# A two-layer mixture kernel: the lower layer's TensorE loop cut from four steps to two and begun two steps early

## The reference, cut to what matters

```python
def reference(x, ctx_1024, ...):                 # x: 32 x 64 x 512, ctx: 32 x 1601 x 512, all float32
    x = x + cross_attention(layernorm(x), ctx_1024)
    x = x + self_attention(layernorm(x))         # 16 heads, causal
    return x + ffn(layernorm(x))

def kmoe(x_flat, W_router, A, B, scale, bias, d_in1, d_in2, d_out1, d_out2, top_k):
    logits = x_flat @ W_router.T                 # 64 experts
    vals, idx = jax.lax.top_k(logits, top_k)     # top_k = 2
    probs = jax.nn.softmax(vals, axis=-1)
    xs = x_flat.reshape(-1, d_in1, d_in2)
    Y = jnp.einsum('nkoi,nij,nkpj->nkop', A[idx], xs, B[idx])
    out = jnp.einsum('nkop,nk->nop', Y, probs).reshape(-1, d_out1 * d_out2)
    return out * scale + bias

def ffn(x):                                      # x.reshape(-1, 1024): 1024 tokens of 32 x 32
    h = kmoe(x, W_up, ..., 32, 32, 64, 64, 2)    # the upper layer: 32 x 32 -> 64 x 64
    h = jax.nn.gelu(h, approximate=False)
    return kmoe(h, W_down, ..., 64, 64, 32, 32, 2)   # the lower layer: 64 x 64 -> 32 x 32
```

## Time and profile before

| | us |
|---|---|
| median of 3 runs (lowest, highest) | 1310.11 (1308.2, 1310.57) |
| the profiled execution | 1309.42 |
| its span in the profile | 1307.6 |
| PE busy in the span | 1223.3 (94%) |
| DVE busy | 802.9 (61%) |
| ACT busy | 440.8 (34%) |
| POOL busy | 277.3 (21%) |

### The profile page before, as it was taken

One profiled execution on the slowest core, in us unless ns is written; L12 is line 12 of the kernel. 1 busy time (PEld: TensorE's weight loads), 2 busy tenths in 40 slices (PEclk: granted clock), 3 DMA queues, 4 the chain that ended last, 5 costly groups with the idle time before them and its releaser, 6 DMA issues.

```text
span 1307.6 us, 63760 instructions
## 1 busy us (share of the span) xinstructions
PE 1223.3 (94%) x28879; PEld 803.6 (61%) x28879; DVE 802.9 (61%) x1603; ACT 440.8 (34%) x894; POOL 277.3 (21%) x470
## 2 busy tenths in 40 slices
PE   9999999999999999999999999786898989789995
PEld 6864333333333333776667766566787878689995
DVE  5566677777777672465555656364756657357774
ACT  2323211321122112221222212225555537257772
POOL 1100000000000001121222212014352515236663
PEclk9999999999999999999999999899999999989996
DMA  8887999899989992411011110400412203644333
GB/s 296 283 258 231 306 298 307 276 314 299 313 268 319 300 305 65 109 65 64 1 65 64 64 48 0 130 34 34 161 65 96 90 39 154 230 166 113 113 65 65
DMA packets 66133, 211.56 MB, mean 162 GB/s; under 512 B 12240, under 2 KB 28624, under 8 KB 51568
## 3 DMA queue, kind: packets, MB, share of 16 engines
q1 hardware_dynamic: 66032, 210.16, 48.6%
HBM read 172.37 MB, written 37.75 MB: 161 GB/s over the span
## 4 chain that ended last, share of the span: by engine, by line
PE 81%; DVE 9%; issue 4%; POOL 2%; ACT 1%; DMA 1%; SPq 1%; POOLq 0%; DVEq 0%; ACTq 0%
PE ps L714 14%; PE ps L563 10%; PE ps L1087 8%; PE ps L2244 5%; DVE arena L575 5%; PE ps L2276 5%; PE ps L2195 5%; PE ps L235 4%; PE ps L1201 4%; PE ps L1108 4%; PE ps L478 3%; PE ps L2173 2%; PE ps L704 2%; PE ps L2289 2%; PE ps L2230 2%
## 5 line engine op out<-in xcount | busy, mean ns | idle before, releaser
L575 DVE STREAM_TRANSPOSE arena<-arena 128x448 f32<-128x448 f32 (+1 forms) x512 | 263.4, 578 | 98.5 <-PE ps L563 79.5
L563 PE MATMUL ps<-arena 32*64 32x400 f32 (+1 forms) x4096 | 202.8, 506 | 2.6 <-DVE arena L575 1.8
L714 PE MATMUL ps<-arena 128*64 128x512 f32 x832 | 189.2, 598 | 0.0
L563 PEld LDWEIGHTS ps<-arena 32*64 32x64 f32 x4096 | 74.9, 130 | 99.5 <-issue 50.7
L714 PEld LDWEIGHTS ps<-arena 128*64 128x64 f32 x832 | 55.5, 136 | 121.3 <-issue 112.0
L598 ACT ACTIVATE arena<-ps,arena 128x384 f32<-128x384 f32 x64 | 36.3, 582 | 276.4 <-DVE arena L589 276.4
L1087 PE MATMUL ps<-arena 128*128 128x256 f32 x512 | 115.3, 383 | 0.8 <-ACT arena L1022 0.8
L1087 PEld LDWEIGHTS ps<-arena 128*128 128x128 f32 x512 | 97.3, 192 | 17.5 <-issue 3.3
L887 POOL TENSOR_TENSOR arena<-arena 128x1024 f32<-128x1024 f32 x8 | 19.0, 2370 | 405.7 <-PE ps L714 405.7
L2091 ACT COPY arena<-ps 128x512 f32<-128x512 f32 x128 | 75.1, 587 | 75.5 <-PE ps L2244 49.1
L1922 DVE SCALAR_TENSOR_TENSOR arena<-ps,arena 128x512 f32<-128x512 f32 x64 | 69.9, 1117 | 38.3 <-PE ps L2230 37.9
(11 more groups left out here) (161 smaller groups left out, 1895.0 us busy)
## 6 DMA issues: line engine op xcount, KB each, us to landing
arena<-ctx SPq DMA_DIRECT2D x64, 1024.0 KB
arena<-ctx SPq DMA_DIRECT2D x32, 768.0 KB
arena<-q_n SPq DMA_DIRECT2D x64, 256.0 KB, 11.2
h_n<-arena SPq DMA_DIRECT2D x16, 1024.0 KB, 4.4
arena<-h_n SPq DMA_DIRECT2D x16, 1024.0 KB, 7.8
arena<-x SPq DMA_DIRECT2D x16, 512.0 KB, 4.3
arena<-ctx SPq DMA_DIRECT2D x32, 256.0 KB
x_n<-arena SPq DMA_DIRECT2D x16, 512.0 KB, 3.5
```

The lines of the kernel that those rows point to most:

```text
L563: last = pe.matmul(ps[b * SEQ:(b + 1) * SEQ, tb, 0:WIDTH[tb]], qs[p % 2][r, db, b * SEQ:(b + 1) * SEQ], z[r, at % RING, b, 0:WIDTH[tb]], s ...
L575: vec.transpose(z[:, at % RING, :, g * 224:g * 224 + nt * 32].rearrange("p b (j t) -> p b j t", t=32), slots[slot_of(k)][:, :, 0:nt, db * ...
L714: last = pe.matmul(ps[b * SEQ:(b + 1) * SEQ, OB, :], probt[:, j, b * SEQ:(b + 1) * SEQ], slot[:, b, jj, :], start=j == 0, stop=j == TILES - 1)
```

## The change

- **Main loop of the lower layer.** The four-step body becomes a two-step body, run 7 and then 21 times, over steps -2 to 53. `first_dn(0)` and `first_dn(1)` are no longer written out ahead; the loop begins two steps earlier, and its first two `second_dn` work on nothing. 56 of the 64 units lie in the loop; it is left when the last is gathered. Then come four laps of two steps without units (three before).
- **Early units.** `EARLY` is 8; they run as a loop of two laps of four (`unit_first`) over four pairs of banks, from slots that POOL stages, the two factors in turn. `transpose_choices` of group 2 comes after all of them, and PE waits there for both copies of it before the logits.
- **Slots.** In the main loop POOL's `stage_unit` uses two slots in turn instead of four.
- **`h`.** The groups 0 to 2 are all loaded into `hb`, group 0 right after the last gather of the upper layer, the later pieces one by one as the steps free their places. Group 3 is neither stored nor loaded: `stage_h` reads it where it is.
- **Transposes.** In the upper layer the second transpose is cut into four pieces of 8 columns, after the gather units of `q` = 1, 2, 3 and 4.
- **Group 0.** `output_stats`, `residual_out`, `normalised_out` and POOL's `rstd` stand ahead of the 16 steps.

PE, the whole of the lower layer, before: nine written-out units around the eight transposes, logits, the two `first_dn` (L2244 x64), the fold, then the body of four steps.

The core of the diff:

```diff
-    h_of = [hb, h, hb, h]
+    h_of = [hb, hb, hb, h]
-    HALF_STEPS, UNITS, EARLY = 8, 64, 9
+    HALF_STEPS, UNITS, EARLY = 8, 64, 8
...
+        sp.wait_ge(s_hd, 64 * (T_N - 1))
+        sp.wait_ge(s_gu, 16 * T_N)
+        sp.wait_ge(s_xt, 8 * T_N)
+        for q in (0, 1, 3):
+            load_h(0, q)
         sp.wait_ge(s_stx, STEPS * T_N + AHEAD)
-        for q in range(4):
-            load_h(0, q)
-        sp.wait_ge(s_hd, 16 * 4 * T_N)
+        load_h(0, 2)
+        sp.wait_ge(s_sth, PIECE + UP + AHEAD - 2)
+        load_h(1, 0)
         sp.wait_ge(s_lgd, T_N)
         load_x2(0)
         load_x2(1)
-        for q in range(4):
-            load_h(1, q)
...
-                if T and q == 1:
-                    transposed(vec, T, 1)
+                if T and 1 <= q <= 4:
+                    transposed(vec, T, 1, q - 1, 4)
...
+            if T == 0:
+                rest.output_stats(vec)
+                rest.residual_out(vec)
+                rest.normalised_out(vec)
...
-                with pe.Fori(lap * 3, lap * 11 + 3) as i:
-                    for b, g in enumerate((1, 2, 3, 0)):
-                        second_dn(i * 4 + b, b % 2)
-                        unit_dn(i * 4 + b, g)
-                        first_dn(i * 4 + b + 2, b % 2)
+                with pe.Fori(lap * 7, lap * 21 + 7) as i:
+                    for b in range(2):
+                        second_dn(i * 2 + b - 2, b)
+                        unit_dn(i * 2 + b - 2, b)
+                        first_dn(i * 2 + b, b)
...
-            with pe.Fori(28, 31) as i:
+            with pe.Fori(28, 32) as i:
...
-        for j in range(EARLY):
-            if j == 2:
-                pe.wait_ge(s_bias, T_N * STEPS + CREDIT)
-            if j == 6:
-                transpose_choices(pe, "dn", 6, T_N - 1)
-            unit_early(j)
+        with pe.Fori(0, 2) as p:
+            for b in range(4):
+                unit_first(p, b)
+        units_out(pe, EARLY - 1)
+        transpose_choices(pe, "dn", 4, T_N - 1)
         for e in range(2):
             pe.wait_ge(s_ohe["dn"][e], 3 + CREDIT)
         pe.wait_ge(s_gelu, T_N * STEPS)
+        units_out(pe, EARLY)
         logits_dn(6)
-        units_out(pe, EARLY)
-        first_dn(0, 0)
-        first_dn(1, 1)
-        fold_dn(T_N, 5)
-        pe.wait_ge(s_oc, UP + AHEAD)
+        fold_dn(T_N, 3)
         steps_dn()
```

More of the change, by code:

```diff
@@ L1300, in mixture_parts @@
     s_wr, s_x2, s_end, s_hd = sem("mo_wr"), [sem(f"mo_x2{u}") for u in range(2)], sem("mo_end"), sem("mo_hd")
-    s_h, s_hf = [sem(f"mo_h{u}") for u in range(2)], [sem(f"mo_hf{u}") for u in range(2)]
+    s_h = [sem(f"mo_h{q}") for q in range(4)]
     s_xf, s_lgu, s_lgd, s_lgb = sem("mo_xf"), sem("mo_lgu"), sem("mo_lgd"), sem("mo_lgb")
@@ L1356, in units_out @@
         for s in s_ged:
-            e.wait_ge(s, count + UP + AHEAD - 8)
+            e.wait_ge(s, count + UP + AHEAD - 9)
     def four(tile):
@@ L1433, in weigh, with transposed @@
                           ALU.mult).then_inc(s_ohp[k], 1)
-    def transposed(vec, T, t):
+    def transposed(vec, T, t, k=0, pieces=1):
         vec.wait_ge(s_x3, 32 * T + 32)
@@ L1672, in mixture @@
     s_hd = first.s_hd
-    s_h, s_hf = first.s_h, first.s_hf
+    s_h = first.s_h
     s_xf = first.s_xf
@@ L1869, in _ @@
             stage_a(T, 1)
+            if T == 0:
+                rest.rstd(pool)
             for n in range(STEPS):
@@ L1877, in _ @@
                     exponential("dn", T - 1)
-                if n == 8 and T == 0:
-                    rest.rstd(pool)
             if T + 1 < T_N:
                 stage_table(T + 1, 0)
-        stage_b_dn(0)
-        stage_b_dn(1)
-        for j in range(EARLY, EARLY + 3):
+        for j in range(EARLY):
             stage_unit(j)
+        stage_unit(EARLY)
         stage_choices(EARLY)
[L1887 to L1892, removed]
+        for s in range(-2, STEPS * T_N):
+            j = s + 2 + EARLY
+            if j + 1 < UNITS:
+                stage_unit(j + 1)
+                if j % 4 == 3:
+                    stage_choices(j + 1)
             if s == 5:
@@ L2032, in _ @@
         for j in range(EARLY):
-            if j == 6:
-                one_hot_out(vec, "dn", T_N - 2, 1, 7)
             gather_out_dn(j)
+        one_hot_out(vec, "dn", T_N - 2, 1, 5)
         stage_h(0)
+        parts(T_N, 6)
+        logits(vec, "dn", T_N - 1, 3)
         stage_h(1)
-        parts(T_N, 6)
-        logits(vec, "dn", T_N - 1, 5)
-        stage_h(2)
-        for s in range(STEPS * T_N):
-            if s + 3 < STEPS * T_N:
+        for s in range(-2, STEPS * T_N):
+            j = s + 2 + EARLY
+            if 2 <= s + 3 < STEPS * T_N:
                 stage_h(s + 3)
-            y_out(s)
-            if s + EARLY < UNITS:
-                gather_out_dn(s + EARLY)
+            if s >= 0:
+                y_out(s)
+            if j < UNITS:
+                gather_out_dn(j)
             if s >= HALF_STEPS:
@@ L2112, in stage_a_dn @@
             if s % HALF_STEPS == 0:
-                units_out(act, s + 4)
+                units_out(act, s + 4 if s else 7)
             act.wait_ge(s_s1, UP + s - 1)
@@ L2247, in first_dn, with unit_first @@
             last.then_inc(s_s1, 1)
-        def unit_early(j):
-            T, cols, v, g = half_of(j)
-            if j >= 3:
-                units_out(pe, j - 2)
-            x = choices_of(j)
+        def unit_first(p, b):
+            pe.wait_ge(s_td, p * 4 + b + 1 + UP + AHEAD - 10)
+            for s in s_ged:
+                pe.wait_ge(s, p * 4 + b - 3 + UP + AHEAD - 9)
+            if b == 2:
+                pe.wait_ge(s_bias, T_N * STEPS + CREDIT)
+            apart(pe, SPARE)
+            x = choices_of(b)
             for o in range(4):
```

128 lines of the change are left out of this document (62 added, 66 removed).

## The result

| | before | after |
|---|---|---|
| runs, median | 1309.34 us (1308.2 to 1310.57, 4 runs) | 1288.43 us (1285.93 to 1289.51, 4 runs) |
| profiled execution, its time and span | 1309.42, 1307.6 us | 1285.93, 1284.1 us |
| PE / DVE / ACT / POOL busy | 94% / 61% / 34% / 21% | 94% / 63% / 34% / 21% |

The ratio is 0.9839, with a 95% interval of 0.9825 to 0.9854: 21 us faster, 1288.4 where 1288.5 was predicted.

A forecast was written before the change was run, and what follows sets the result against it. PE was taken to bound the kernel (81% of the span). Terms 2.8 + 2.9 - 0.2 + 11.5 + 0 + 2.0 + 2.6 = 21.6 us gave 1287.8, or 1288.5 us as median, with a range of 1283 to 1298.

The forecast's parts named there:

- group 0's steps: Upper layer: moving DVE's four steps and POOL's rstd ahead of group 0's steps saves 2.8 us (1.5 to 3.4).
- transposes in four pieces: Gathers of groups 1 to 3: the 0.98 us wait for DVE's copy goes, saving 2.9 us (1 to 3.6).
- beginning, first unit to `second_dn(0)`: Lower layer's start: 25.2 us against 25.0 before, a loss of 0.2 us (-4 to +2).
- steps 0 to 11: Lower layer's main loop: 26.9 us instead of 38.4, as its code is loaded already; saves 11.5 us (8 to 12).
- steps 11 to 13: Around the transposed choices in the lower layer: 9.0 us with the same waits as before, so no change.
- step 13 to the loop's end: Main loop: 101.5 us against 103.5, 2.46 a step and left two steps earlier; saves 2.0 us (0 to 3).
- steps without units: Last steps, 54 to 63: 13.2 us instead of 15.8, without code wait or half clock; saves 2.6 us (-5 to +3).
- The count of code: PE waits once per about 63 written-out matmuls; first unit to loop's end, five boundaries instead of nine, loop turns free.
- branch rival: Main loop: each of 28 turns waits for code, 0.60 to 2.31 us, giving 1305 to 1353 us; chance 0.04.
- The length of the waits: Early lower layer: the longest code waits (3.49, 2.31 us) fall while h loads; 1.5 us allowed for the body's two boundaries.
- The half clock, the likeliest rival: Steps without units run at half clock, 20.0 us instead of 13.2, giving 1295.5 us; chance 0.15.
- The slots: Main loop: with two slots POOL's copies delay PE; at 2.85 us a step, 1311 us and more; chance 0.04.

The follow-up runs named there:

- run with the lap written out: Changed kernel with the first 14 steps of the lower layer's main loop (-2 to 11) written out instead of seven loop turns; 1.0037 of the kernel before.
- second burst run: Changed kernel plus four 1 MB stores of the last h, ahead of group 1's first h load in SP's queue; 0.9867 of the kernel before.
- two upper-layer runs: Kernel before with only the second transpose of groups 1 to 3 in four pieces (0.9971), or only group 0's DVE steps and POOL's rstd moved ahead (0.9976).
- first burst run: Changed kernel plus four 1 MB stores of the last h, behind the load that waits for step 3 in SP's queue; 0.9849 of the kernel before.
- four-step run with late loads: Changed kernel with a four-step body, SP holding the loads of h and x2 until step 7 is staged; 0.9837 of the kernel before.

## Why the prediction was right, step by step

| term | predicted | measured |
|---|---|---|
| group 0's steps | +2.8 | +3.0 |
| transposes in four pieces | +2.9 | +3.4 |
| beginning, first unit to `second_dn(0)` | -0.2 | +0.3 |
| steps 0 to 11 | +11.5 | +11.6 |
| steps 11 to 13 | 0 | +1.5 |
| step 13 to the loop's end | +2.0 | +2.3 |
| steps without units | +2.6 | +2.3 |
| end | 0 | +0.15 |
| elsewhere ahead of the first unit | 0 | -1.1 |

The measured column is between the two profiled executions and adds up to their 23.5 us. "Elsewhere" is 0.4 us by which the steps of group 0 started later, 0.45 by which the first unit waited longer for issue (1.05 or 1.06 in every profile with the changed beginning, 0.60 in the four with the old one; why was not settled), and 0.3 in small pieces. "Group 0's steps" goes to the next gather; the steps alone, as the prediction counted them, gave 3.4 (25.3 us instead of 28.7), and 0.3 of it went in the longer wait behind them.

**The count of code** was the step on which the rest hung, and it held: boundaries at a fixed spacing, each paid once, four blocks fewer, none for the turns. The run with the last loop written out confirmed it by place, with an offset of five matmuls that I can't explain. The queue's packets confirmed it by number. (The branch rival lets the body span three boundaries; by the prediction's own count it is two, and nothing in the sum rests on that.)

**The length of the waits** was attributed rightly to the loads of `h` (runs with loads held back, and with a burst). The prediction's 1.5 us for the two boundaries in the body was too much; there was one of 0.58. Its idea of why the change gains 11.5 us is incomplete, though. The runs divide it: holding the loads back, alone, makes the kernel 6.4 us faster (4.7 to 8.2 by the interval) and leaves four waits of 4.5 us together in that stretch, which fewer blocks take away. The kernel before could have had about half of these 11.5 us with one wait in SP's queue.

**Steps 11 to 13** is the miss in the list, and it is not the change's doing. Eleven profiles transpose the choices ahead of step 12. In ten of them PE then waits 1.63 or 1.67 us (0.96 in the run with the lap written out). Of these ten, two had the clock fall behind it (9.03 us from step 11 to 13: the kernel before and the second burst run), eight did not (7.5 us).

**Luck.** What steps 0 to 11 cost in the kernel before varies from execution to execution as well. PE's lower-layer code and the loads are the same in the kernel before and in the two upper-layer runs, which needed 38.4, 35.1 and 36.8 us. From the first unit to `second_dn(13)` the three took 72.5, 68.5 and 70.6 us, the changed kernel 59.0 in both its profiles. So that stretch gained 13.4, 9.5 or 11.5, where the prediction's three terms add up to 11.3. It had read the slowest of the three and yet came out at their mean of 11.5: against that mean, steps 0 to 11 were put 1.6 too high, the beginning 1.2 and steps 11 to 13 0.5 too low. As far as three profiles tell, the before's slow one is also why the profiled pair differs by 23.5 us and the medians by 21. The mechanism and most terms were right within 0.5 us; that the total lies within 0.1 us of the median, in a measurement good to 2.6, is luck.

**The signs.** All that the prediction named as "right" came (group 0's steps 25.3, 24.7 to `second_dn(0)`, 26.8 for the next eleven, 2.47 a step, clock 1.00 at the end) but one: waits for DVE of 0.61 and 0.62 us are left in the gathers of groups 2 and 3. They stood there before (0.65 and 0.63) and are not the one that the pieces removed.

**Main loop and last steps** went as worked out: 101.2 where 101.5 was worked out, and 13.5 where 13.2 was. The half clock, the likeliest rival, stayed away because the wait ahead of it did: two runs that put a wait back there, one of them without touching these steps, had it again. The slots were priced at 0.04 and were further off than that. The branch rival fell: loops over two to five blocks turned without a packet.

**Small misses in the beginning.** "POOL's staging of eight units is hidden": the profile puts 0.52 us at the turn of the loop of units down to POOL's copy. That unit's own copy had ended at 1100.25, 3.6 us earlier, so the name is doubtful and the 0.52 may be the turn of that loop. It wasn't settled. The copies behind the transposes (0.67, for 0.8) and of the parts (0.55, in 1.2) came near.

**Not run alone** are the loop of early units, and group 3's `h` left out of store and load. The first burst run stores those 4 MB again, later and with the same time (0.9849), so the store at least was not on PE's path.

## What to carry to other kernels

Count the written-out instructions of the busiest engine from stall to stall: waits "for issue" at a constant spacing, once per place, are code being loaded, and the packets of the queue "instruction" give the number of blocks. Such a load queues with your own DMAs, so keep bulk transfers out of the stretch in which an engine first enters new code; here a single wait in the DMA-issuing queue gave 6.4 us, and the shorter loop body gave nothing once that wait was there. And compare several profiles of the same code before you give a stretch with a fallen clock a price.

## What the runs showed of the hardware

- A block of code that nothing delays is there about 3.5 to 4.0 us after the one before it was entered: with the DMA engines idle (share 0.02), PE resumed at 1122.87, 1126.64 and 1130.66 in the four-step run with late loads, and at 1135.03, 1138.86, 1142.40 and 1146.21 in the kernel before with its loads held back. With four 1 MB stores ahead of it, one block took PE 5.01 us of waiting; with 2 MB of loads 3.68.
- PE keeps more code than I had reason to assume. From 1160 to 1250 us the changed kernel's instruction queue q8 has no packet at all, although each turn crosses two boundaries, and the four-step body turned as freely over four. The Trainium skill, "Runtime: NRT & Kernel Launch", Instruction fetch mechanics, gives PE 128 KiB of instruction memory in one sentence and two lines of 16 KiB in another. The runs agree with the first as far as they go, and disagree with the second. Its block of 256 instructions agrees with the 16 KB packets.
- The clock's fall behind a wait is not fixed by the wait's length. The same wait of 1.63 or 1.67 us was followed by half clock twice in ten profiles. The waits of 3.29, 3.49, 3.68, 3.76 and 5.01 us in the lower layer's loops were each followed by it; at a sixth, 3.32 in the run with group 0 reordered, the clock was at half already when the wait began.
- Shorter waits: 0.93 to 1.47 us in the main loop left the clock at 1.00 in the two runs with the loads held back, but in two others waits of 1.29 and 1.37, each behind several more, were followed by half clock. In the last steps a wait of 1.10 to 1.80 us was followed by 0.50 in all six profiles that have one there (1.10, 1.21, 1.26, 1.53 and twice 1.80), and the clock did not come back before `second_dn(63)`.
